# A wait for the scan of state k ahead of GpSimd's product for state k+3, in the state space stage of a two-layer decoder

## The chip, the cores and the metric

The kernel runs on one core of a Trainium2 chip. Its time is the device time of one execution in microseconds (us); the median of several runs is compared. A core has five engines with queues of their own: TensorE (PE in the profile, its weight loads PEld), VectorE (DVE), ScalarE (ACT), GpSimd (POOL) and SyncE (SP), which here issues DMA. They are ordered only by semaphores.

## The reference, cut to what matters

The whole program is six sub-layers on x of 8 x 256 x 512, each followed by a layer norm of x plus its result: sliding window attention, quantised cross attention, a GELU layer, a selective state space, linear attention, and a mixture of experts. The change is in the state space, and there in the recurrence over the 256 tokens:

```
u = silu(xs);  A = -exp(A_log);  dbc = u @ W_x          # N = 16 states
delta = softplus(dbc[..., :dtr] @ W_dt + b_dt)
deltaA = exp(einsum('bld,dn->lbdn', delta, A))
deltaBu = einsum('bld,bln->lbdn', delta * u, Bm)
h = dA * h + dBu;  y_t = einsum('bdn,bn->bd', h, c)      # one step over tokens
y = ys.transpose(1, 0, 2) + u * D;  out = y * silu(r);  return out @ W_out + xs
```

## The kernel before, in words

The kernel goes through eight stages one after another; the state space is the sixth (`state_space`). It handles the 8 batches in a software pipeline. In one step n there are 16 iterations k, one for each of the 16 states of batch n; the other parts of the work (convolution and projections of the batches behind, gate, output and norm of the batch before) are spread in pieces over the same 16 iterations. Channels lie on the 128 partitions in KD = 4 groups, tokens along the row, so a tile is 128 x 1024 numbers in float32. States are counted through over all batches as c = 16 n + k (`chunk_of`), 128 in all.

Each state takes this way through the engines:

- ScalarE computes `decay[c]`, exp(delta times a), in 4 activations (L2185), up to two states ahead of the scan.
- GpSimd computes the driving term, du times b (`drive`, L2335), and writes it into `state[c % 4]`. In iteration k it issues the product for state k+3 (`DRIVE_LEAD` = 3).
- VectorE runs the scan over the tokens (L2383), reading `decay` and `state` and writing the state in place. It waits for both.
- TensorE transposes the scanned state into PSUM (`turn`, L1933), in two halves of four transposes; in its order, the transposes of state k-1 come at the beginning of iteration k, ahead of that iteration's piece of the projections.
- VectorE adds the transposed state times c to an accumulator in two halves (L2394, `add_up`); in iteration k it does so for state k-2, right after scan k.

The state tiles form a ring of RING = 4. So the product for state c may overwrite its tile only when the transposes of state c-4 have been read from it; that is the wait on `turn_ready` in `drive`, which is there for all states from the fifth on. `scanned` is raised by each scan's end; until now TensorE and ScalarE wait for it.

Other work stands in the same queues. GpSimd in iteration 2 multiplies the accumulator of the batch before by its gate (L2346), and in iteration 11 computes the norm's inverse root and offsets (L82, L2358). VectorE in iterations 8 and 10 forms y (L2410) with its statistics (L1754), after iteration 10 also the moments, and at the end of iteration 12 makes delta (L2420) and du (L2423) for the next batch; the first product of that batch waits for du. Each engine runs its instructions strictly in the order written. `g.sem_inc(waited, 1)` behind a wait is only the instruction that carries the wait.

Of the kernel before, what the change touches and what calls it, by code (L numbers as in the profile page):

```python
# [35 lines left out]
ONE = 1  # L36
# [42 lines left out]
def inverse_root(g, ln, n):  # L79

    g.wait_ge(ln.shifted_ready, ONE + n + 1)
    g.tensor_tensor(ln.rstd[:, :], ln.shifted[:, :], ln.minus_half[:, :], ALU.pow).then_inc(ln.rstd_ready, 1)  # L82
# [17 lines left out]
def flat(a):  # L100

    return a.rearrange("p a b -> p (a b)")


def spread(row, n):

    return row.rearrange("p (o d) -> p o d", o=1).to_broadcast([P, n, row.shape[-1]])
# [1588 lines left out]
def state_space(nc, A, x_in, x_out, hold):  # L1696
# [9 lines left out]
    DRIVE_LEAD = 3  # L1706
    SUM_LAG = 2
    CONV_B, OUT_T, X_T, Y0, DT_B, C_T, Y1, Z, XC, SKIP, XC1, GATE, CONV_A = 0, 1, 3, 5, 6, 7, 8, 9, 11, 12, 14, 15, 17
    with Phase(nc, "ss", "right") as p:
# [108 lines left out]
        def run(eng, step):  # L1818

            step(-1, 0, False, False, False, True)  # L1820
            step(-1, 1, False, False, True, True)
            step(0, 0, False, True, True, True)
            with eng.Fori(0, (B - 4) // 2) as pair:
                step(pair, 1, True, True, True, True)
                step(pair + 1, 0, True, True, True, True)
            h = B // 2
            step(h - 2, 1, True, True, True, True)
            step(h - 1, 0, True, True, True, False)
            step(h - 1, 1, True, True, False, False)
            step(h, 0, True, False, False, False)  # L1830
# [13 lines left out]
        def wait_read(eng, q, s, j):  # L1844
            eng.wait_ge(freed[place(s, j)], ONE + used(q, s, j) + 1)

        def chunk_of(q, s, k):

            return q * (2 * N) + s * N + k
# [462 lines left out]
        @block.gpsimd  # L2312
        def _(g):
            behind.late_pool(g)
            g.memset(ln.minus_half[:, :], -0.5).then_inc(ln.half_set, 1)
            g.wait_ge(ln.half_set, ONE + 1)
            g.wait_ge(consts, ONE + 80)
            for m in range(KD):
                ins = g.tensor_scalar(diag[:, m, :], ident[:, :], skip[:, m:m + 1], None, ALU.mult)
            ins.then_inc(diag_ready, 1)  # L2320

            def step(q, s, post, back, mid, front):
                n = q * 2 + s

                def drive(q, s, k):
                    c = chunk_of(q, s, k)
                    if k == 0:
                        g.wait_ge(du_ready, ONE + q * 2 + s + 1)
                        g.sem_inc(waited, 1)
                        g.wait_ge(b_in, ONE + 16 * (q * 2 + s + 1))  # L2330
                        g.sem_inc(waited, 1)
                    if not (isinstance(q, int) and c < RING):
                        g.wait_ge(turn_ready, ONE + (c - RING + 1) * TB)
                        g.sem_inc(waited, 1)
                    g.tensor_tensor(state[k % RING][:, :, :], du[s][:, :, :], spread(b_all[s][:, k, :], KD), ALU.mult)\  # L2335
                        .then_inc(drive_ready, 1)

                for k in range(N):
                    if k == 2 and post:
                        last = (q - 1, s)  # L2340
                        g.wait_ge(summed, ONE + TB * chunk_of(q, s, 0))
                        g.sem_inc(waited, 1)
                        for t in range(TB):
                            wait_read(g, *last, GATE + t)
                            g.sem_inc(waited, 1)
                        g.tensor_tensor(flat(acc[1 - s][:, :, :]), flat(acc[1 - s][:, :, :]), flat(gate[1 - s][:, :, :]),  # L2346
                                        ALU.mult).then_inc(gated, 1)
                    if k + DRIVE_LEAD < N:
                        if back:
                            drive(q, s, k + DRIVE_LEAD)  # L2350
                    elif mid:
                        drive(q + s, 1 - s, k + DRIVE_LEAD - N)
                    if k == 11 and post and not (isinstance(q, int) and n == B):
                        inverse_root(g, ln, n - 1)
                        g.wait_ge(ln.rstd_ready, ONE + n)
                        g.sem_inc(waited, 1)
                        for t in range(TB):
                            ins = g.tensor_scalar(offset[:, t:t + 1], ln.moments[:, t, 0:1], -1.0, ln.rstd[:, t:t + 1],  # L2358
                                                  ALU.mult, ALU.mult)
                        ins.then_inc(offset_ready, 1)  # L2360

            run(g, step)
# [971 lines left out]
```

## Time and profile before

| | |
|---|---|
| median of 3 runs | 2904.63 us (2903.69 to 2905.1) |
| the profiled execution's own time | 2909.72 us |
| its span, first to last instruction | 2907.4 us |
| busy share of the span | PE 90%, PEld 61%, DVE 68%, ACT 50%, POOL 41% |
| mean granted TensorE clock | 0.964 |
| GpSimd's products (L2335) | 128, 433.3 us, mean 3395 ns |
| VectorE's scans (L2383) | 128, 386.9 us, mean 3023 ns |

The shares are averages over eight stages with different limits. The stage of the change lies between about 1690 and 2335 us. The stages are sequential, so what it gains or loses is gained or lost by the whole. An instruction counts as busy from its start to its end, also when it stands still in between.

### The profile page before, as it was taken

The numbers are of one execution on the slowest core, as the hardware profiler recorded it, in microseconds if no ns is written. First come the engines' busy times: TensorE is split into PE (matmuls) and PEld (weight loads), VectorE is DVE, ScalarE is ACT, GpSimd is POOL, SyncE is SP. The second block draws the span as 40 slices with busy tenths as digits, with TensorE's granted clock in tenths as the row PEclk, the third lists the DMA queues.
The fourth block names the chain that finished last, engine by engine and source line by source line (L and its number), as shares of the span: only waits on it lengthen the run. The fifth ranks groups of instructions, "written<-read, shape, count | busy, mean of one in ns | idle before, by whom it ended". The sixth has DMA issues, their size and how long they took to land. (4 is left out here: it accounts for less than half of the span.)

```text
span 2907.4 us, 47462 instructions
## 1 busy us (share of the span) xinstructions
PE 2623.1 (90%) x16930; PEld 1760.0 (61%) x16941; DVE 1988.6 (68%) x2548; ACT 1459.1 (50%) x2864; POOL 1206.2 (41%) x1148
## 2 busy tenths in 40 slices
PE   8999899988888888887999999999998879998997
PEld 5666655634444444443899777777776555555873
DVE  4788757689999999966121149999999933333544
ACT  3444422279999998972232156666676511111520
POOL 0000026446665665553222137776888810000352
PEclk9999999989999999999999999999999989998899
DMA  2123514268888888975012201111112270120273
GB/s 94 57 91 128 190 56 116 58 134 171 168 164 171 169 167 160 189 161 188 30 39 72 102 37 52 59 59 59 59 52 81 85 130 23 43 81 8 98 153 146
DMA packets 537722, 297.99 MB, mean 102 GB/s; under 512 B 444400, under 2 KB 482544, under 8 KB 533680
## 3 DMA queue, kind: packets, MB, share of 16 engines
q1 hardware_dynamic: 520896, 258.50, 35.4%
q0 software_dynamic: 16624, 36.84, 4.1%
q8 instruction: 122, 2.00, 0.3%
q14 instruction: 80, 0.66, 0.1%
HBM read 126.45 MB, written 64.23 MB: 66 GB/s over the span
## 5 line engine op out<-in xcount | busy, mean ns | idle before, releaser
L1188 DVE TENSOR_REDUCE xh_top<-xh_seen 128x1 f32<-128x512 f32 (+1 forms) x768 | 631.6, 864 | 44.1 <-PE xh_seen L1090 30.5
L1160 ACT ACTIVATE xh_prob<-xh_sc,xh_bias,xh_scale 128x1024 int16<-128x1024 f32 (+1 forms) x512 | 610.1, 1202 | 67.4 <-PE xh_sc L1090 67.1
L2335 POOL TENSOR_TENSOR ss_state<-ss_du,ss_b_all 128x1024 f32<-128x1024 f32 x128 | 433.3, 3395 | 185.2 <-PE ss_turned L1933 110.8
L1090 PE MATMUL xh_seen<-xh_kT,xh_qT 96*128 96x512 bf16 x1024 | 353.3, 387 | 80.4 <-DVE xh_top L1188 78.1
L2383 DVE TENSOR_TENSOR_SCAN ss_state<-ss_decay,ss_state 128x1024 f32<-128x1024 f32 x128 | 386.9, 3023 | 28.7 <-ACT ss_decay L2185 28.7
L1090 PE MATMUL xh_sc<-xh_kT,xh_qT 96*128 96x512 bf16 x1024 | 308.1, 383 | 1.4 <-ACT xh_prob L1160 1.3
L1214 POOL CAST xh_probT<-xh_pairs 128x2048 int16<-128x2048 uint8 x128 | 242.1, 1891 | 12.6 <-DMA xh_pairs<-xh_prob 3.8
L1090 PEld LDWEIGHTS xh_seen<-xh_kT,xh_qT 96*128 96x128 bf16 x1024 | 89.2, 97 | 240.8 <-DVE xh_top L1188 219.2
L1940 PE MATMUL ss_bank<-ss_xc,hold_w_conv 128*128 128x256 f32 x1024 | 229.3, 379 | 0.7 <-ACT ss_xc L2197 0.7
L2185 ACT ACTIVATE ss_decay<-ss_delta,ss_a 128x255 f32<-128x255 f32 x512 | 210.7, 496 | 0.4
L1940 PEld LDWEIGHTS ss_bank<-ss_xc,hold_w_conv 128*128 128x128 f32 x1024 | 190.0, 189 | 26.4 <-ACT ss_xc L2197 1.1
L1114 PEld LDWEIGHTS xh_o<-xh_v_head,xh_probT 128*128 128x128 f16 x4096 | 133.9, 96 | 84.5 <-POOL xh_probT L1214 38.8
L1228 POOL TENSOR_SCALAR xh_low<-xh_top 128x1 f32<-128x1 f32 x256 | 93.1, 364 | 207.4 <-DVE xh_top L1188 206.9
L2394 DVE SCALAR_TENSOR_TENSOR ss_acc<-ss_turned,ss_c_t,ss_acc 128x512 f32<-128x512 f32 x256 | 176.4, 729 | 1.1 <-PE ss_turned L1933 1.1
L1933 PE MATMUL ss_turned<-ss_ident,ss_state 128*128 128x128 f32 x1024 | 138.6, 277 | 34.8 <-DVE ss_acc L2394 33.1
L1933 PEld LDWEIGHTS ss_turned<-ss_ident,ss_state 128*128 128x128 f32 x1024 | 118.8, 143 | 60.5 <-DVE ss_state L2383 30.3
L1114 PE MATMUL xh_o<-xh_v_head,xh_probT 128*128 128x32 bf16 x4096 | 142.3, 177 | 14.3 <-DVE xo_heads_out L1177 8.3
L1090 PEld LDWEIGHTS xh_sc<-xh_kT,xh_qT 96*128 96x128 bf16 x1024 | 96.1, 98 | 77.3 <-ACT xh_prob L1160 4.6
L82 POOL TENSOR_TENSOR la_rstd<-la_shifted,la_minus_half 128x2 f32<-128x2 f32 x8 | 5.6, 694 | 318.9 <-DVE la_shifted L71 318.9
L1676 DVE TENSOR_TENSOR gf_e<-gf_y_psum,gf_b 128x1024 f16<-128x1024 f32 x8 | 9.8, 1225 | 185.0 <-PE gf_y_psum L1631 185.0
L1616 PE MATMUL gf_hid_psum<-gf_xT,gf_w 128*128 128x256 f32 x1024 | 126.6, 286 | 8.8 <-POOL gf_xT L1574 8.8
L1616 PEld LDWEIGHTS gf_hid_psum<-gf_xT,gf_w 128*128 128x128 f32 x1024 | 126.3, 195 | 9.8 <-issue 9.2
(399 smaller groups left out, 4767.8 us busy)
## 6 DMA issues: line engine op xcount, KB each, us to landing
ex_rows_in<-sa_unused POOLq DMA_DIRECT2D x18, 1088.0 KB, 5.2
ss_b_all<-ss_states SPq DMA_DIRECT2D x8, 2048.0 KB, 7.2
xa_kT<-xp_kT SPq DMA_DIRECT2D x8, 768.0 KB, 5.2
xh_qT<-xa_qT SPq DMA_DIRECT2D x48, 128.0 KB, 3.2
xh_kT<-xa_kT SPq DMA_DIRECT2D x48, 128.0 KB, 3.4
sa_x<-in_x SPq DMA_DIRECT2D x8, 512.0 KB, 3.8
sa_y<-in_x SPq DMA_DIRECT2D x8, 512.0 KB, 6.6
x_after_self_attention<-sa_y_out SPq DMA_DIRECT2D x8, 512.0 KB, 6.1
```

The lines of the kernel that those rows point to most:

```text
L1090: ins = pe.matmul(out[:, c * D:(c + 1) * D], qT[s][:, t * P:(t + 1) * P], kT[s][:, at + c * D:at + (c + 1) * D], start=True, stop=True)
L1114: ins = pe.matmul(o[:, t, :], probT[t % RING][:, b, :].bitcast(F16), v_head[s][:, b, :], start=(b == 0), stop=(b == TT - 1))
L1160: act.activation(out, scores, ACT.Exp, bias=bias[t % RING][:, :], scale=scale[s][:, t:t + 1], accum_out=total[s][:, half, t:t + 1]).then_i ...
L1188: ins = v.tensor_reduce(top[t % RING][:, k:k + 1], scores[:, 0:n], AX.X, ALU.max)\
L1214: g.tensor_copy(probT[t % RING][:, :, :].rearrange("p (b two) q -> p b two q", two=2), pairs[t % RING][:, :, :].bitcast(U8).rearrange("p b ...
L1616: ins = pe.matmul(hid_psum[m // 2 % 3][:, m % 2, :], w0[i][:, c, m * P:(m + 1) * P], xT[:, c, :], start=(c == 0 and i == 0), stop=(c == KD ...
L1933: ins = pe.transpose(turned[r][:, m * P:(m + 1) * P], state[k % RING][:, m, t * P:(t + 1) * P], ident[:, :])
L1940: ins = pe.matmul(out, w_conv[:, k, c, m * P:(m + 1) * P], xc[:, c, k:k + S], start=(k == 0 and c == 0), stop=(k == TAPS - 1 and c == KD - 1))
L2185: ins = act.activation(decay[k % RING][:, m, 1:], delta[s][:, m, 1:], ACT.Exp, scale=a[:, m, k:k + 1])
L2335: g.tensor_tensor(state[k % RING][:, :, :], du[s][:, :, :], spread(b_all[s][:, k, :], KD), ALU.mult)\
L2383: v.tensor_tensor_scan(flat(state[k % RING][:, :, :]), flat(decay[k % RING][:, :, :]), flat(state[k % RING][:, :, :]), 0.0, ALU.mult, ALU. ...
L2394: v.scalar_tensor_tensor(acc[s][:, t, :], turned[(k * TB + t) % BANKS][:, :], c_t[s][:, t, k:k + 1], acc[s][:, t, :], ALU.mult, ALU.add).t ...
```

## The change

The product for state c, from the fifth state on, waits for a second thing: that the scan of state c-3 has ended. With c = k+3 in iteration k, that is the scan of the same iteration on VectorE. The wait has its own carrying instruction.

```diff
@@ -2332,6 +2332,8 @@
                     if not (isinstance(q, int) and c < RING):
                         g.wait_ge(turn_ready, ONE + (c - RING + 1) * TB)
                         g.sem_inc(waited, 1)
+                        g.wait_ge(scanned, ONE + c - DRIVE_LEAD + 1)
+                        g.sem_inc(waited, 1)
                     g.tensor_tensor(state[k % RING][:, :, :], du[s][:, :, :], spread(b_all[s][:, k, :], KD), ALU.mult)\
                         .then_inc(drive_ready, 1)
```

## Rows read from the trace of the kernel before

**Rows 1.** Windows of one 16-state period; us, busy by engine, clock, DMA.

```profile
1783.50:1863.40 79.90, 77.22 (x418) 61.94 (x417) 75.20 (x59) 53.76 (x111) 53.91 (x21) 1.00 0.14 54
1941.95:2021.70 79.75, 77.13 (x417) 61.59 (x416) 75.20 (x59) 53.48 (x110) 54.44 (x21) 1.00 0.14 54
2100.20:2178.70 78.50, 75.45 (x410) 60.48 (x409) 75.08 (x59) 52.06 (x107) 65.37 (x21) 1.00 0.13 48
```

**Rows 2.** Waits from 1700 to 2330 us: total, times, longest.

```profile
POOL ss_state L2335 <- PE ss_turned L1933: 110.8, 52, 6.0
PE ss_turned L1933 <- DVE ss_acc L2394: 33.1, 17, 3.1
DVE ss_state L2383 <- ACT ss_decay L2185: 28.7, 16, 3.5
```

**Rows 3.** VectorE in order of time: start, us, instruction, idle before and releaser.

```profile
1881.57 3.68 DVE L2383 TENSOR_TENSOR_SCAN ss_state<-ss_decay,ss_state 128x1024 f32<-128x1024 f32 x1 [1.66 <-ACT ss_decay L2185]
1900.76 4.05 DVE L2383 TENSOR_TENSOR_SCAN ss_state<-ss_decay,ss_state 128x1024 f32<-128x1024 f32 x1 [1.29 <-ACT ss_decay L2185]
```

**Rows 4.** The scan's line: shortest, median, longest ns; then its group.

```profile
L2383 DVE TENSOR_TENSOR_SCAN ss_state<-ss_decay,ss_state x128: 2259/3087/4460, 1704.5 to 2325.2; 128x1024 f32<-128x1024 f32 x128
L2383 DVE TENSOR_TENSOR_SCAN ss_state<-ss_decay,ss_state 128x1024 f32<-128x1024 f32 x128 | 386.9, 3023 | 28.7 <-ACT ss_decay L2185 28.7
```

**Rows 5.** VectorE in order of time, 1907 to 1930 us.

```profile
1907.47 2.27 DVE L2383 TENSOR_TENSOR_SCAN ss_state<-ss_decay,ss_state 128x1024 f32<-128x1024 f32 x1
...
1910.96 3.10 DVE L2383 TENSOR_TENSOR_SCAN ss_state<-ss_decay,ss_state 128x1024 f32<-128x1024 f32 x1
...
1917.41 2.29 DVE L2383 TENSOR_TENSOR_SCAN ss_state<-ss_decay,ss_state 128x1024 f32<-128x1024 f32 x1
...
1925.24 3.40 DVE L2420 TENSOR_TENSOR ss_delta<-ss_delta,ss_soft 128x1024 f32<-128x1024 f32 x1
1928.67 1.23 DVE L2423 TENSOR_TENSOR ss_du<-ss_delta,ss_u 128x1024 f32<-128x1024 f32 x1
```

**Rows 6.** GpSimd in order of time, 1876 to 1931 us.

```profile
1876.42 4.35 POOL L2346 TENSOR_TENSOR ss_acc<-ss_acc,ss_gate 128x1024 f32<-128x1024 f32 x1
...
1909.09 2.81 POOL L2335 TENSOR_TENSOR ss_state<-ss_du,ss_b_all 128x1024 f32<-128x1024 f32 x1 [2.12 <-PE ss_turned L1933]
1914.29 2.37 POOL L2335 TENSOR_TENSOR ss_state<-ss_du,ss_b_all 128x1024 f32<-128x1024 f32 x1 [2.38 <-PE ss_turned L1933]
...
1925.18 2.37 POOL L2335 TENSOR_TENSOR ss_state<-ss_du,ss_b_all 128x1024 f32<-128x1024 f32 x1
1930.42 3.84 POOL L2335 TENSOR_TENSOR ss_state<-ss_du,ss_b_all 128x1024 f32<-128x1024 f32 x1 [2.87 <-DVE ss_du L2423]
```

**Rows 7.** GpSimd in the first batch: the first product issued early.

```profile
1732.06 2.37 POOL L2335 TENSOR_TENSOR ss_state<-ss_du,ss_b_all 128x1024 f32<-128x1024 f32 x1 [1.96 <-PE ss_turned L1933]
```

**Rows 8.** The last batch: a backlog, the last early product, a long scan.

```profile
2270.26 28.23 POOL L2335 TENSOR_TENSOR ss_state<-ss_du,ss_b_all 128x1024 f32<-128x1024 f32 x7
2308.45 4.21 POOL L2335 TENSOR_TENSOR ss_state<-ss_du,ss_b_all 128x1024 f32<-128x1024 f32 x1 [1.34 <-PE ss_turned L1933]
2316.03 4.46 DVE L2383 TENSOR_TENSOR_SCAN ss_state<-ss_decay,ss_state 128x1024 f32<-128x1024 f32 x1
```

**Rows 9.** TensorE's transposes, 1913 to 1935 us.

```profile
1913.07 1.04 PE L1933 MATMUL ss_turned<-ss_ident,ss_state 128*128 128x128 f32 x8
...
1932.80 1.97 PE L1933 MATMUL ss_turned<-ss_ident,ss_state 128*128 128x128 f32 x8 [2.21 <-DVE ss_acc L2394]
```

**Rows 10.** A product just ahead of a scan, batch 1.

```profile
1830.94 2.36 POOL L2335 TENSOR_TENSOR ss_state<-ss_du,ss_b_all 128x1024 f32<-128x1024 f32 x1 [3.88 <-PE ss_turned L1933]
1831.04 4.40 DVE L2383 TENSOR_TENSOR_SCAN ss_state<-ss_decay,ss_state 128x1024 f32<-128x1024 f32 x1
```

**Rows 11.** delta and du with VectorE first, 2239 to 2245 us.

```profile
2239.91 1.21 DVE L2420 TENSOR_TENSOR ss_delta<-ss_delta,ss_soft 128x1024 f32<-128x1024 f32 x1
2241.15 3.26 DVE L2423 TENSOR_TENSOR ss_du<-ss_delta,ss_u 128x1024 f32<-128x1024 f32 x1
```

## The prediction

> **What bounds the kernel now.** I read the stages by window first, because the change touches only one of the eight stages, the state space; it runs from about 1704 to 2335 us and handles 8 batches of 16 states. Three windows of one 16-state period each [rows 1] last from 78.5 to 79.9 us, with VectorE busy for 75.1 to 75.2 us, TensorE for 75.5 to 77.2, GpSimd for 54 to 65. Two engines are close to full, so busy time does not say which one sets the pace. The waits do [rows 2]: TensorE waits 33.1 us for VectorE's sums in 17 places, VectorE only 28.7 us for ScalarE's decays, and GpSimd 110.8 us for TensorE's transposes. The pace passes between them inside each batch. From about scan 8 of a batch to scan 13 VectorE runs without a gap and TensorE ends up waiting for it; from scan 14 to about scan 4 or 8 of the next batch TensorE runs without a gap and VectorE has spare time, which shows as its idle of 1.66 and 1.29 us ahead of two scans [rows 3].
>
> Next the durations, because VectorE's "busy" is partly waiting. One scan form, one shape, lasts from 2.26 to 4.46 us [rows 4], and one product form on GpSimd from 2.36 to 4.21 [rows 8, 10]. Followed in order of time, they exclude each other. The scan at 1907.47 meets no running product and takes 2.27 us, to 1909.74. The product that was issued inside it at 1909.09 ends at 1911.90, 2.16 us after that scan's end, though a product with nothing beside it takes 2.37 (1914.29). The next scan is issued at 1910.96, 0.94 us before that product's end, and lasts 3.10 us, to 1914.06: 2.16 us after the product's end [rows 5, 6]. So whoever comes second stands still, with its time counted as busy, until the first is done. The two sums between scans take the 1.22 us from 1909.74 to 1910.96 and do not care. A period is therefore scan, then product, with the sums hidden beside the product: 3.10 + 1.22 = 4.32 us. A scan met by nothing would be 2.27, and 128 of them are 96 us less than the 386.9 of [rows 4].
>
> **What the change does, step by step.** Nothing is removed and no DMA moves. GpSimd gets one more wait and one more counter increment ahead of each product from the fifth on, 124 in all. The product for state k+3 may now start only when scan k has ended.
>
> (1) *The products that this holds back.* I compared each product's start with the end of the scan it will wait for. In 57 cases the product is issued before that end, as at 1909.09 against 1909.74 [rows 5, 6]; the first such is at 1732.06, the last at 2308.45 [rows 7, 8]. In the other 67 the product is later anyway, held by the transposes or by its predecessor on GpSimd: after the gate product (L2346) GpSimd is one scan behind and runs seven products back to back, 28.23 us, 4.03 each [rows 8]. For these the scan named is already over, and the new wait is passed at once.
>
> (2) *The price of one that is held back.* It loses the place that it had while standing behind the scan. Now it ends 2.16 us after the scan. Afterwards the counter has to reach GpSimd and the whole instruction has to run. A product released by TensorE at 1914.11 (1913.07 + 1.04) starts at 1914.29, 0.18 us later [rows 6, 9]; released by VectorE's du at 1929.90 through three waits in a row it starts at 1930.42, 0.52 later, so some 0.17 per wait [rows 5, 6]. New end: 0.18 + 2.37 = 2.55 us after the scan, 0.39 us later than now. The next scan's length follows the product's end one to one, so 3.10 becomes 3.49 and the period 4.32 becomes 4.71. Bounds: 0 if a held product is taken as fast as a standing one; 0.56 (0.39 + 0.17) if the additional wait is paid after the scan too. I take 0.39, the row for one wait, because the older wait has been passed by then.
> Of the 57, 50 have a next scan that stands behind them; for the other 7 VectorE has y's sum and statistics in between (from 1914.06 to 1917.41, 3.35 us [rows 5]), which hides all of it. All 50 on the path would be 50 x 0.39 = 19.5 us.
>
> (3) *What of it lies on the path.* By batch the 50 are 8, 8, 5, 8, 5, 5, 5, 6.
> - First batch: VectorE has no spare time from scan 5 on, so 8 x 0.39 = 3.1 us.
> - Batches 2, 4, 5, 6: three of the five stand at scans 14, 15 and 0, where TensorE sets the pace; their 1.17 us go into the 1.66 us idle [rows 3]. The two at scans 10 and 12 are on the path: 0.78. But with scans 1.17 us later, the gate product ends later too, at about 1881.9 in place of 1880.77 (1876.42 + 4.35 [rows 6]), past the 1881.57 at which the scan is ready, and then GpSimd's catching up with two products in the gap no longer fits. That puts a part back. Between 0.78 and 5 x 0.39 = 1.95 I take 1.2 each, together 4.8.
> - Batches 1 and 3: five on the path, 1.95, less one gain: the product at 1830.94 starts 0.10 us before its scan (1831.04), which lasts 4.40 for it [rows 10]. With VectorE 1.5 us later by then, the product falls inside the scan before, stands there, and the scan is 3.1: 1.3 back. 0.7 each, together 1.4.
> - Last batch: little TensorE work, VectorE is waited for, 6 x 0.39 = 2.3. Its scan at 2316.03 comes 0.05 us after a product and lasts 4.46 [rows 8]. If the additional wait turns this order, 1.4 are saved; as even odds, 0.7. Leaves 1.6.
> Sum 3.1 + 4.8 + 1.4 + 1.6 = 10.9 us.
>
> (4) *Small ones.* Where products are back to back (seven in 28.23 us, nothing idle between [rows 8]) GpSimd passes its waits while the instruction before runs, and one more costs nothing. Where the transposes release the product the wait adds up to 0.17, some 15 times, 2.6 us if all of it were on the path; I take 0. At delta (L2420) product and VectorE tie: the product (1925.18) starts 0.06 us before it and delta lasts 3.40 with du 1.23, sum 4.63; in the batch at 2239.91 VectorE came first and the pair is 1.21 + 3.26 = 4.47 [rows 5, 6, 11]. Turning that tie gives 0.16 us a batch, below 1 us in all; 0. TensorE's idle grows by about 1 us at scan 13. After such a wait at 1932.80 the eight transposes took 1.97 us in place of 1.04, the lower of the clock's two levels [rows 9]; the batch that follows took 79.75 us against 78.50 for another [rows 1]. At none to four more such falls: 0 to 4.8 us; I take 0.
>
> **One rule weighed.** The rows show that the second of the two stands until the first is done. The Trainium skill, "SBUF — State Buffer", section "Who interferes with whom", says the same: the one that issues second is blocked completely until the other has finished. Taken literally this speaks for no cost at all: a product kept back until the scan's end loses nothing, as it was blocked until then, and the sum would be 0. By the rows the standing product ends 0.39 us earlier than a fresh one would, and the sum is 10.9.
>
> **The rivals.**
> *No change (2904.6; between 2898.8 and 2910.4).* About 0.2% is what a measurement of this kernel can tell, 5.8 us. Either the 0.39 is near 0 since a standing product is no faster than a fresh one, or idle of VectorE (28.7 us in all, some 3 a batch) takes the rest: 8 x 0.78 = 6.2 us would be left. For it: TensorE is at 96% of a batch. Against it: it waits for VectorE in every batch.
> *Faster (2896).* The mechanism is the order at near ties: a product that starts just before a scan costs it a whole product. 18 scans last over 3.5 us, together 72.1, which is 16.3 over 18 x 3.10. If delaying products and scans turns half of them, 8.2 us go: 2904.6 - 8.2 = 2896.4. It decides where a product starts less than 0.2 us ahead of a scan (0.10 us in one case, 0.05 in another [rows 8, 10]). Against it: most of the 18 are caused by GpSimd's backlog or by transposes, and the new wait starts nothing earlier.
> *Everything on the path and the clock with it (2929).* 19.5 + 4.8 = 24.3 us. For it: the two alternate without a gap, so that time in which neither runs is hard to get back.
> That the change does nothing because the wait is always passed already is excluded by the 57.
>
> **Numbers.** Forecast +10.9 on the profiled execution's 2909.72 gives 2920.6 (span 2907.4, to 2918.3); the median of the runs is 5.1 us below the profiled time, so 2904.63 + 10.9 = 2915.5 us. Chances: slower by my sum or thereabouts (2910.4 to 2924) 0.58, no change 0.27, faster 0.08, everything on the path 0.07. Range for 8 in 10: 2904 to 2926, of which the likeliest case's own is 2911 to 2922. Slower by over 0.2%: 0.65.
>
> **What would show it.** In the profile after: no product begins inside the scan that it is held by, so long products (3.5 to 4.4 us) grow rarer while GpSimd waits for the scan (L2383), a releaser that is absent now; a group of scans at 3.4 to 3.5 us beside those at 3.1; the scans' total up by more than 10 us; gaps of about 0.18 us from scan's end to product's start. Batches of some 79 to 80 us. The forecast is wrong if scans keep at 3.1 us behind a held product (price), if VectorE's idle for the decays shrinks by as much as the scans grow (cover), or if the number of scans over 3.5 us falls by half (order).

## The result, and the profile after

The changed kernel is slower: median 2924.83 us (2920.53 to 2932.93, 4 runs) against 2904.86; the medians are 20.0 us apart, the ratio is 1.0073, 95% interval 1.0049 to 1.0096. In a second measurement of the same kernel it is 1.0059 (1.0038 to 1.0079). The direction was forecast, the size was not: I had 10.9 us, these ratios are 21 and 17. The profiled execution took 2920.53 us, its span is 2918.6.

Other stages scatter by more than this change is worth (from the first to the last matmul of the experts it is 213 to 218 us in nine of the seventeen profiles of this document, 230 to 247 in the other eight), so I read the stage itself: from the start of the first scan to the start of the last it took 620.7 us before and 636.3 after; in a second profile of each, 618.6 and 634.8. That is 15.9 us on average, 0.55% of the kernel, inside both intervals.

The two groups and the waits of the stage in the kernel after, as in [rows 2, 4]; the line numbers are two higher from the added lines on.

```profile
L2385 DVE TENSOR_TENSOR_SCAN ss_state<-ss_decay,ss_state 128x1024 f32<-128x1024 f32 x128 | 402.1, 3142 | 28.8 <-ACT ss_decay L2185 28.7
L2337 POOL TENSOR_TENSOR ss_state<-ss_du,ss_b_all 128x1024 f32<-128x1024 f32 x128 | 379.9, 2981 | 253.9 <-DVE ss_state L2385 146.1 <-DVE ss_du L2425 54.8 <-PE ss_turned L1933 53.0
```

```profile
POOL ss_state L2337 <- DVE ss_state L2385: 146.1, 53, 4.7
PE ss_turned L1933 <- DVE ss_acc L2396: 39.4, 17, 3.5
DVE ss_state L2385 <- ACT ss_decay L2185: 28.7, 14, 3.4
```

GpSimd's line looks better by 53 us (433.3 before), and that is no gain: time in which it stood behind scans, counted as busy, is now shown as waiting for them, in 53 places. (Of the 146.1 us of that wait another part was a wait for the transposes before, which fell from 110.8 to 53.0.) The line that counts is VectorE's: its scans are 15.2 us longer in sum. Its idle for the decays is the same 28.7 us in this pair of profiles. In the second pair the scans are 22.1 us longer and that idle falls from 28.0 to 23.2, so there spare time did take some of it; the stage grows by about 16 us in both. TensorE waits longer for VectorE (39.4 against 33.1).

The same place as [rows 5], in order of time: VectorE of the kernel after, then GpSimd.

```profile
1914.34 2.27 DVE L2385 TENSOR_TENSOR_SCAN ss_state<-ss_decay,ss_state 128x1024 f32<-128x1024 f32 x1
...
1917.83 3.48 DVE L2385 TENSOR_TENSOR_SCAN ss_state<-ss_decay,ss_state 128x1024 f32<-128x1024 f32 x1
...
1932.88 3.39 DVE L2422 TENSOR_TENSOR ss_delta<-ss_delta,ss_soft 128x1024 f32<-128x1024 f32 x1
```

```profile
1887.59 21.94 POOL L2337 TENSOR_TENSOR ss_state<-ss_du,ss_b_all 128x1024 f32<-128x1024 f32 x6
...
1916.79 2.37 POOL L2337 TENSOR_TENSOR ss_state<-ss_du,ss_b_all 128x1024 f32<-128x1024 f32 x1 [2.58 <-DVE ss_state L2385]
...
1932.81 2.38 POOL L2337 TENSOR_TENSOR ss_state<-ss_du,ss_b_all 128x1024 f32<-128x1024 f32 x1
```

The scan at 1914.34 ends at 1916.61; the product starts at 1916.79, 0.18 us later, and ends at 1919.16, 2.55 us after the scan. The scan issued at 1917.83 lasts 3.48 in place of 3.10. After the next scan there is y's work in between, and the scan behind it (1924.66) takes 2.29 as before: nothing lost. The six products from 1887.59 stand back to back as before. At delta the product still comes 0.07 us first. Over all 128 scans, 47 now last 3.4 to 3.5 us (none before), 38 last 3.0 to 3.15 (76 before), and 12 last over 3.5 (18 before). In the second pair of profiles the first two counts are much the same (45 against 1, 37 against 77), but the third is 17 against 16.

TensorE at the end of that batch, beside [rows 9]:

```profile
1940.43 1.97 PE L1933 MATMUL ss_turned<-ss_ident,ss_state 128*128 128x128 f32 x8 [2.38 <-DVE ss_acc L2396]
1942.19 4.27 PE L2071 MATMUL ss_bank<-hold_w_in,ss_xT 128*128 128x512 f32 x8
```

It has waited, and the granted clock is at its lower level (1.2 of 2.4 GHz): 0.51 in the mean from 1940.1 to 1943.5. The transposes take 1.97 in place of 1.04, the matmuls behind them 4.27 in place of the 3.60 of the same eight in `after_busy2`, where the clock is not lowered.

**The stage by batch.** The table is the time from the start of scan 13 of one batch to that of the next, worked out from VectorE's rows in order of time; the first column runs from the first scan to scan 13 of batch 0, the last from scan 13 of batch 6 to the last scan of all. "Middle" is the sum of the six between, taken before they are rounded. A star marks a batch in which the clock fell to 1.2 GHz right at its start (in the last part it falls in every profile).

```
                   first   0-1   1-2   2-3   3-4   4-5   5-6    last   middle  whole
before              66.9  79.9* 78.6  79.7* 78.6  78.5  77.8    80.9   472.9   620.7
before, again       66.9  78.6  79.8* 78.5  78.5  78.5  77.8    79.9   471.7   618.6
after               71.1  80.4* 80.4* 80.4* 80.5* 79.5  80.3*   83.6   481.6   636.3
after, again        71.0  80.4* 79.7  80.6* 79.6  80.3* 79.4    83.6   480.1   634.8
```

### The profile page after: what moved, and what is told of

Read it like the earlier page. It is cut to its first block and busy times, and to the rows that moved or that the text cites. A ratio compares the mean times of both kernels' runs of the same rounds, so it can differ in the third digit from the quotient of the medians.

```text
span 2918.6 us, 47659 instructions
## 1 busy us (share of the span) xinstructions
PE 2629.8 (90%) x16941; PEld 1763.4 (60%) x16941; DVE 2003.7 (69%) x2548; ACT 1458.4 (50%) x2864; POOL 1151.5 (39%) x1148
## 5 line engine op out<-in xcount | busy, mean ns | idle before, releaser
L1160 ACT ACTIVATE xh_prob<-xh_sc,xh_bias,xh_scale 128x1024 int16<-128x1024 f32 (+1 forms) x512 | 609.8, 1202 | 67.3 <-PE xh_sc L1090 66.9
L2337 POOL TENSOR_TENSOR ss_state<-ss_du,ss_b_all 128x1024 f32<-128x1024 f32 x128 | 379.9, 2981 | 253.9 <-DVE ss_state L2385 146.1
L2385 DVE TENSOR_TENSOR_SCAN ss_state<-ss_decay,ss_state 128x1024 f32<-128x1024 f32 x128 | 402.1, 3142 | 28.8 <-ACT ss_decay L2185 28.7
L1933 PE MATMUL ss_turned<-ss_ident,ss_state 128*128 128x128 f32 x1024 | 142.2, 282 | 41.5 <-DVE ss_acc L2396 39.4
```

What stands on the lines that cost most here:

```text
L1160: act.activation(out, scores, ACT.Exp, bias=bias[t % RING][:, :], scale=scale[s][:, t:t + 1], accum_out=total[s][:, half, t:t + 1]).then_i ...
L1933: ins = pe.transpose(turned[r][:, m * P:(m + 1) * P], state[k % RING][:, m, t * P:(t + 1) * P], ident[:, :])
L2385: v.tensor_tensor_scan(flat(state[k % RING][:, :, :]), flat(decay[k % RING][:, :, :]), flat(state[k % RING][:, :, :]), 0.0, ALU.mult, ALU. ...
```

## The experiments

Each is told by the whole and by the parts of that table, since a few us in the stage are 0.1 to 0.3% of the kernel, near what the ratios can tell. The kernel before had medians of 2904 to 2931 us in these measurements, and not by the chip alone (chip 11 gave 2925.2 once and 2904.3 once); each ratio is against its runs in the same measurement.

**The change once more** (`again`, nothing edited).

> The changed kernel, unaltered, in more runs. The state space stage of its profile grew by about 16 us (from 2325.25 to 2340.76 at the last scan, with both traces laid on the first scan, and 1.0 before that), the median by 20. Theory: the held products cost 0.39 each and the rest above 16 us is scatter of the granted clock, so a median of 2917 to 2925 and a lowest near 2919. Rival (TensorE's longer idle brings regular falls of its clock, an effect of its own): runs spread from 2919 to 2933 with the granted clock falling from 0.963 to 0.957 as the time grows.

Ratio 1.0059 (1.0038 to 1.0079), 634.8 us in the stage. The stage repeats within 1.5 us. The median expected cannot be held against the 2944.13 measured, since the kernel before took 2925.24 there. Nor does the rival's pattern show: the six runs lie between 2943.0 and 2949.7, the granted clock between 0.956 and 0.961 in no order with them, and the kernel before scatters from 2919.7 to 2937.5 in this measurement too.

**The kernel before once more** (nothing edited).

> The kernel before, unaltered, for a second profile. Every theory: 620 to 622 us from first to last scan, as in the first profile (620.7), no scans at 3.4 to 3.5 us. If it is off by more than 1 us, differences of that size between batches mean nothing.

Ratio 1.0002 (0.9988 to 1.0017), 618.6 us in the stage: 2.1 under the first profile, a little more than the 1 us expected. The table says where: a fall of the clock in one middle batch in place of two, and 1.0 in the last part. There the near tie of [rows 8] has turned by itself: with nothing changed, the scan of state 13 of the last batch lasts 3.07 us in place of 4.46. The product that it meets, issued at 2316.14, comes while the scan before still runs (2314.52 to 2316.79) and stands behind that one.

```profile
2318.02 3.07 DVE L2383 TENSOR_TENSOR_SCAN ss_state<-ss_decay,ss_state 128x1024 f32<-128x1024 f32 x1
```

So differences of 1 us in a single batch are read only together with the stars, and against the mean of the two profiles.

**A wait that is always passed.**

```diff
-                        g.wait_ge(scanned, ONE + c - DRIVE_LEAD + 1)
+                        g.wait_ge(scanned, ONE + c - RING + 1)
```

> The added wait asks for the scan of state c-4 in place of c-3; the wait on the transposes of c-4 already implies it, so it is always passed and only its instructions are left. Theory (the price lies in giving up the place behind the scan): 0 to +2.6 us, products again issued inside the scan, scans at 3.08. Rival (the instructions themselves on GpSimd's queue cost it): more than half of the 20 us.

Ratio 0.9994 (0.9980 to 1.0008), 621.1 us in the stage, scans' median 3085 ns. The instructions of the wait do take time on GpSimd: behind a release by the transposes the product starts 0.28 or 0.34 us after it in place of 0.18. But nothing of this reaches the stage; a product that stands behind a scan ends 2.16 us after it all the same (the one at 1909.45 lasts 2.65 us, its like at 1909.09 in [rows 6] 2.81). What costs is what the added wait waits for.

**The wait for some states only.** `only_0_1_2`, `only_3_15`, `only_12_15`: the two added lines under `if k < 3:`, `if k >= 3:` or `if k >= 12:`, k being the product's own state.

> The added wait only for states 0, 1, 2 of a batch, whose products stand behind scans 13, 14 and 15. The prediction put these three under TensorE's pace: 0 to +2 us in all. Rival (they are on the path like the others): 3 x 7 x 0.39 = 8.2 us.

> The added wait for states 3 to 15 alone. The prediction: nearly all of the change's cost is here, +9 to +16 us. Rival (states 0 to 2 are on the path): +6 to +10, the two halves adding up to the whole.

> The added wait only for states 12 to 15, whose products stand behind scans 9 to 12, in the stretch that VectorE paces. The changed kernel is 15.6 us longer from first to last scan; states 3 to 15 alone gave 12.3, states 0 to 2 alone 3.0. Theory (only what stands in VectorE's stretch counts in the middle batches): two held products a batch on the path, 8 batches x 0.75 = 6 us, so 626 to 628 with middle batches 0.8 longer. Rival (place does not matter; every held product costs 0.39 wherever it is): the same number here, but then states 0 to 2 should have cost 7.8 rather than 3.0; it is told apart by the middle batches, which must then be no more than 0.8 longer in the changed kernel per two held.

```
                   first   0-1   1-2   2-3   3-4   4-5   5-6    last   middle  whole   ratio (95%)
states 0 to 2       66.9  79.0  79.7  79.0  79.0  79.7  78.3    82.0   474.7   623.7   1.0031 (1.0016-1.0047)
states 3 to 15      71.0  80.8  79.3  80.8  79.3  80.7  78.5    82.4   479.6   633.0   1.0053 (1.0034-1.0072)
states 12 to 15     68.3  79.3  79.3  80.1  79.3  79.2  80.1    81.7   477.4   627.4   1.0035 (1.0018-1.0053)
```

Against the mean of the two profiles before (619.7; first 66.9, middle 472.3, last 80.4) states 0 to 2 add 4.0 us and states 3 to 15 add 13.3; the whole change adds 15.9, so the two are nearly additive. States 0 to 2 hold back 21 products, 8.2 us worth at 0.39, and 4.0 arrive: 2.4 us in the middle batches, for 18 held products, and the rest in the last part. That the 18 lie under TensorE's pace in part was right, though 0 to 2 us was too low. States 12 to 15 add 7.7, of which 5.1 in the six middle batches, 0.8 each: two held products on the path. The forecast had 0.78. In the last part all three kernels have the near tie of [rows 8] as the first profile before has it (the scan lasts 4.45 to 4.46), so it is that profile's 80.9 that they compare with: before rounding, +1.2 for three held products, +1.5 for four, +0.8 for two, and +2.7 for seven in the whole change. There every held product costs its full 0.39. The three ratios are wider than these differences.

**The wait written twice.** The two added lines stand twice in a row, so that a product that was held back starts later still.

> The changed kernel with the added wait and its increment written twice, so that one more instruction lies between the scan's end and the product. From first scan to last the state space took 620.7 us before and 636.3 changed. Theory (the price is the time from the scan's end to the product's start, paid by the next scan): product 0.35 after the scan in place of 0.18, scans of 3.64 in place of 3.47, and some 45 x 0.17 = 7.7 us on top of 636 where on the path, 2 to 7 counting what idle hides. Rival (the cost is the loss of the order, whatever the delay): no more than 1 us on top.

GpSimd, then VectorE, of this kernel, first batch (the last row is the last batch's):

```profile
1738.59 2.36 POOL L2339 TENSOR_TENSOR ss_state<-ss_du,ss_b_all 128x1024 f32<-128x1024 f32 x1 [2.42 <-DVE ss_state L2387]
```

```profile
1734.76 3.56 DVE L2387 TENSOR_TENSOR_SCAN ss_state<-ss_decay,ss_state 128x1024 f32<-128x1024 f32 x1
...
2336.33 2.28 DVE L2387 TENSOR_TENSOR_SCAN ss_state<-ss_decay,ss_state 128x1024 f32<-128x1024 f32 x1
```

The additional wait puts the product 0.27 us after the scan's end (1738.32), not 0.35: one more costs 0.09 us here, not the 0.17 that I had from du. Scans take 3.56. The stage takes 638.6 us in the one profile (ratio 1.0073, 1.0055 to 1.0091, from two runs), 18.9 over before and 3.0 over the changed kernel, where 2 to 7 were expected. So the price per held product went from 0.39 to 0.48 and the cost from 15.9 to 18.9 us: 15.9 / 0.39 = 41 and 18.9 / 0.48 = 39. The cost goes with the delay, and some 40 held products' worth of it are on the path. In the last part the tie has turned here (the scan at 2336.33 lasts 2.28, that of the changed kernel 4.45; the next one 3.08 in place of 2.28), which gives 1.4 us back: 82.9 is less than the 83.6 of the changed kernel in spite of the higher price.

**TensorE kept busy in its idle.** Four (`busy`) or two (`busy2`) additional matmuls, whose result is overwritten by the gate's projection, ahead of the transposes of iteration 14; in the changed kernel and in the one before.

```diff
+                    if k == 14 and mid:
+                        out = fill(GATE + 1)
+                        for c in range(KD):      # range(2) in busy2
+                            pe.matmul(out[:, :], xT[1 - s][:, c, P:2 * P], w_in[:, c, D:2 * D], ...)
                     if k > 0 and back:
                         turn(q, s, k - 1)
```

> The changed kernel, and TensorE does four additional matmuls of 128x512 in iteration 14 ahead of its transposes, where it waits about 3 us for VectorE; what they write is overwritten by the gate's projection. They fill the idle after which its clock falls. Theory (clock): fewer low stretches than the 9 of the changed kernel in this stage and batches of 79.5 in place of 80.4 us, first to last scan 632 to 634. Rival (the clock costs nothing, VectorE alone sets the pace): 636 as before, however the clock stands.

> The kernel before with the same four matmuls. Theory (clock): the two batches of 79.7 and 79.9 us that follow a fall go to 78.6, first to last scan 618 to 619 in place of 620.7. Rival: unchanged, or longer by up to 1 us a batch if the matmuls outlast the idle of 2.2 us.

> The changed kernel with two additional matmuls of 128x512 (1.8 us) on TensorE ahead of the transposes of iteration 14, where it waits 2.4 us or more; what they write is overwritten. The six middle batches take 480.0 to 481.5 us in the changed kernel, 478.1 with four matmuls. Clock theory: 1 us or less of idle is left, no fall there, transposes at 1.04 us, batches all at 79.3 to 79.6, sum 476 to 478. Rival (VectorE alone sets the pace): 480 to 481.

> The kernel before with the same two matmuls. Its six middle batches take 471.7 and 473.1 us in two profiles, with one or two of them at 79.8 where the rest are at 78.5. Clock theory: none at 79.8, sum 470 to 471.5. Rival (the additional work delays TensorE, as four matmuls did: 476.1): above 473.

```
                   first   0-1   1-2   2-3   3-4   4-5   5-6    last   middle  whole   ratio (95%)
after, four         74.4  79.9  79.6  79.9  79.7  79.6  79.4    83.5   478.1   636.1   1.0051 (1.0033-1.0070)
before, four        70.4  79.2  79.3  79.7  79.4  79.3  79.2    79.9   476.0   626.4   1.0030 (1.0020-1.0040)
after, two          71.6  79.7  79.7  80.0  79.7  79.6  79.4    83.6   477.9   633.1   1.0050 (1.0029-1.0072)
before, two         68.6  78.6  78.6  78.6  78.6  78.5  77.8    80.0   470.5   619.1   0.9991 (0.9979-1.0002)
```

The added matmuls of the changed kernel, four and then two (each counts as two in the rows), and the transposes behind the two:

```profile
1938.12 3.60 PE L2158 MATMUL ss_bank<-hold_w_in,ss_xT 128*128 128x512 f32 x8
```

```profile
1936.70 1.88 PE L2158 MATMUL ss_bank<-hold_w_in,ss_xT 128*128 128x512 f32 x4
1939.77 1.31 PE L1933 MATMUL ss_turned<-ss_ident,ss_state 128*128 128x128 f32 x8 [1.19 <-DVE ss_acc L2401]
```

Four take 3.60 us, which outlasts the idle of the kernel before and costs it 3.7 us in the middle; for that question this pair was badly sized. They also make the first part 3.4 to 3.5 us longer in both kernels, so by the whole both expectations were missed (636.1 for 632 to 634, 626.4 for 618 to 619). The pair with two answers the question for the middle batches: no fall at the start of any of them in either kernel, and none in the kernel before at 79.8. (In the first part two matmuls still cost 1.7 and 0.6 us.) The clock's falls are worth 472.35 - 470.51 = 1.8 us there and 480.87 - 477.94 = 2.9 in the changed kernel (both sums lie where I expected them, the second only just; the transposes took 1.31 and not 1.04, at a granted clock of 1.00). The difference of the two kernels without falls is 477.94 - 470.51 = 7.4 us; with them it is 480.87 - 472.35 = 8.5. So in the middle batches the clock explains 1.1 us of the loss, and VectorE the rest. The first part has a fall of its own, of which more below.

**The gate product on VectorE**, in the kernel before: L2346 with its waits taken out of GpSimd's iteration 2 and put at the end of VectorE's iteration 1.

> The kernel before, with the gate product moved from GpSimd (iteration 2, L2346, 4.35 us) to VectorE (end of iteration 1), where it should take 1.2 us plus what it stands behind a product. Theory (scans and products share one place, and GpSimd's backlog after the gate makes the long scans at 3.7 and 4.0 us): backlog gone, fewer than 18 scans over 3.5 us, first to last scan 5 to 10 us under 620.7, all of it 0.2 to 0.4%. Rival (VectorE is full, so anything put there costs): 7 x 2 = 14 us longer.

Ratio 1.0001 (0.9990 to 1.0012), 619.6 us in the stage, 17 scans over 3.5 us. Both were wrong: it costs nothing and gains nothing that can be measured. The backlog is gone, and with it the long scans 4 and 8 (3.68 and 4.05 us in batch 2), but in the same batches scans 2 and 10 are long now (4.43 and 3.98). The collisions have moved.

**The product for state 15 behind du**, in the kernel before; then with the gate product on VectorE too; then in the changed kernel.

```diff
+                    if k == 12 and mid and back:
+                        g.wait_ge(du_ready, ONE + n + 2)
+                        g.sem_inc(waited, 1)
                     if k + DRIVE_LEAD < N:
                         if back:
                             drive(q, s, k + DRIVE_LEAD)
```

> The kernel before, with one wait more in each batch but at another place: the product for state 15 (iteration 12) waits for du, so that it no longer starts 0.06 us before delta and costs it 2.2 us. Theory (scans, delta, du and products take turns, and a product is free only where VectorE leaves a gap): delta 1.2 in place of 3.4, the product goes behind scan 13; 1 to 2 us less in a batch, 7 to 14 in all, 0.2 to 0.5%. Rival (the turn is only moved): the product pushed back makes a backlog that costs the same 2.2 at scans 14 to 2, so 0 to -2 us in all.

> The same with the gate product on VectorE too, so that the product pushed back does not meet GpSimd's backlog of the gate. That move alone gave 1.1 us from first to last scan. Theory: backlog gone, 10 to 18 us less than before from first to last scan. Rival: TensorE, busy 75.5 of 78.5 us in a batch, sets the pace as soon as VectorE is quicker, so no more than 3 us.

> The changed kernel, and the product for state 15 waits for du as well, as in the version that took 608.4 us from first to last scan in place of 619.7. Theory (the price of a held product and the collision at delta are separate): 635.6 - 11.3 = 624, scans at 3.47 still there. Rival (the backlog that follows the pushed product hides the new wait, since a product in a backlog is issued after the end it waits for): most of the price gone too, 612 to 618.

VectorE, then GpSimd, of the first of the three, at the end of iteration 12:

```profile
1919.90 1.21 DVE L2423 TENSOR_TENSOR ss_delta<-ss_delta,ss_soft 128x1024 f32<-128x1024 f32 x1
...
1922.28 2.29 DVE L2386 TENSOR_TENSOR_SCAN ss_state<-ss_decay,ss_state 128x1024 f32<-128x1024 f32 x1
```

```profile
1922.72 21.30 POOL L2335 TENSOR_TENSOR ss_state<-ss_du,ss_b_all 128x1024 f32<-128x1024 f32 x5 [2.84 <-DVE ss_du L2426]
```

```
                   first   0-1   1-2   2-3   3-4   4-5   5-6    last   middle  whole   ratio (95%)
p15_du              66.1  76.6  76.6  76.6  76.6  76.5  77.3    82.2   460.1   608.4   0.9958 (0.9942-0.9974)
p15_du_gate         66.1  76.3  76.6  76.3  76.4  76.2  77.6    82.5   459.4   608.0   0.9971 (0.9958-0.9984)
after_p15           69.8  77.3  77.3  77.9  77.4  77.3  77.2    84.0   464.4   618.2   1.0003 (0.9987-1.0020)
```

The first of the three beats both kernels: 11.3 us less in the stage (7 to 14 were expected), and a ratio 0.42% under 1. Delta takes 1.21 in place of 3.40, and the product pushed back stands behind the next scan, which it costs nothing. The batches lie at 76.6, near TensorE's busy 75.5, and none of the middle ones shows a fall of the clock at its start; by the pair with two matmuls I estimate that the absence of falls is 1.8 of the 11.3 us. The last part is 1.8 us longer. The gate product on VectorE adds nothing to it (11.7 us less, inside the 10 to 18 expected, but none of it by that move). In the changed kernel the same three lines bring 17.4 us (635.6 to 618.2); the held products' price is down from 15.9 to 9.8, with 21 scans at 3.4 to 3.5 us in place of 47. I had 624 with the two separate, or 612 to 618 with the price mostly gone. It is in between, at the edge of the second: in the backlog that follows the pushed product, products are issued after the end that they wait for, and those pay nothing.

## Why the prediction was wrong in its size

- **Step 1, which products are held back: right in kind, one short.** 57 were counted, 50 with a scan behind them. By the rows of the kernel before it is 58 and 51: the last batch has seven such products, not six. The trace after has 53 waits of GpSimd for a scan, and 47 scans of 3.4 to 3.5 us.
- **Step 2, the price: right.** 0.39 was forecast, from 0.18 for the release and 2.37 for a fresh product; 0.18, 2.37 and scans of 3.45 to 3.49 were measured. Of its bounds, 0 is excluded; one more wait costs 0.09 behind a scan's release, but 0.10 or 0.16 behind a release by the transposes, so the 0.17 taken from du was not far off there. With a wait that is passed the stage pays nothing, as step 4 had it. The rule that was weighed, taken literally, gave a cost of 0; for the standing product the rows were right.
- **Step 3, what lies on the path: here it failed.** 10.9 us at 0.39 are 28 held products; the measured 15.9 are 41, and the wait written twice says 39. By its terms:
  - First batch: 3.1 forecast, 4.1 measured. I priced each scan by what it was before. But the scan at 1758.06 lasts 4.28 us (3.23 before): its product was released by TensorE, not by a scan, and no longer early enough, at 1757.80, 0.26 us ahead of the scan. And where the last product meets delta, 0.4 us came on top that I had not followed. TensorE was late there by a fall of the clock that the forecast did not have: it waits 2.95 us for VectorE, the granted clock is 0.50 from 1749.0 to 1752.4 (1.00 before), and eight matmuls take 3.27 us in place of 1.89. Both profiles of the changed kernel have this fall in that wait, and neither of the kernel before has it there (in the second the clock falls at 1757.8, and the part still takes 66.9). 1.4 us earlier the transposes would have been done before the scan ahead of the product ended (1756.84); the product would have started at 1757.02, and the scan would last 3.47 like its neighbours. So by this estimate up to 0.8 of the 4.1 us comes from the clock. No run separates it.
  - Middle batches: 6.2 forecast (4.8 + 1.4), 8.5 measured. Without the falls of the clock it is 7.4. For a range of 0.78 to 1.95 a batch, 1.2 was near, except in batch 6, which is 2.0 longer (1.6 without falls); the term for more falls, which I took as 0, is 1.1 us net, since the kernel before has falls as well. The gain that I had put into batches 1 and 3 came (their scans of 4.40 and 4.32 us last 3.48), but it belongs to the batches that begin with a fall: in the second profile before, the one such batch is batch 2, and the scan of 4.39 is there.
  - Last batch: 1.6 forecast, 3.2 measured, half of it missed. I took six held products less 0.7 for a tie that might turn. There are seven, longer by 0.38 to 0.40 each, 2.7 us, and that is all of 83.6 - 80.9, the difference to the first profile before. The tie did not turn in the changed kernel: the scan is at 4.45 us (4.46 before). But it is not fixed: it had turned in the second profile of the kernel before, which lowers the mean before by 0.5 and makes up the rest of the 3.2, and it has turned with the wait written twice. That I gave it even odds was a guess, and it says nothing on what the wait does.
- **The rivals.** "No change" fails on the price. "Faster" needed near ties to turn. The scans over 3.5 us are 12 in place of 18 in the first pair of profiles, but 17 and 16 in the second, so no drop is shown that repeats; the single gains, as in batches 1 and 3, are in the sum above. "Everything on the path and the clock", 24.3 us, is too much by 8: states 0 to 2 cost about a third of their price in the middle batches, so there is cover. The clock's falls are real: 1.1 us net in the middle, and by the estimate up to 0.8 in the first part, of the 4.8 that I had as their bound.
- **The distance between stage and kernel.** The ratios 1.0073 and 1.0059 mean 21 and 17 us, the stage shows 15.9. Both intervals contain it. Whether 1 to 5 us more lie elsewhere, the runs do not tell.

The rows of the kernel after for the two places named: VectorE's, GpSimd's, and TensorE's of the first place, then the same matmuls of the kernel before:

```profile
1758.06 4.28 DVE L2385 TENSOR_TENSOR_SCAN ss_state<-ss_decay,ss_state 128x1024 f32<-128x1024 f32 x1
...
2332.60 4.45 DVE L2385 TENSOR_TENSOR_SCAN ss_state<-ss_decay,ss_state 128x1024 f32<-128x1024 f32 x1
```

```profile
1757.80 2.39 POOL L2337 TENSOR_TENSOR ss_state<-ss_du,ss_b_all 128x1024 f32<-128x1024 f32 x1 [3.11 <-PE ss_turned L1933]
...
2332.53 2.37 POOL L2337 TENSOR_TENSOR ss_state<-ss_du,ss_b_all 128x1024 f32<-128x1024 f32 x1
```

```profile
1748.25 1.56 PE L1933 MATMUL ss_turned<-ss_ident,ss_state 128*128 128x128 f32 x8 [2.95 <-DVE ss_acc L2396]
1749.61 3.27 PE L1946 MATMUL ss_bank<-ss_u,ss_w_x 128*128 128x256 f32 x8
...
1756.45 2.40 PE L1933 MATMUL ss_turned<-ss_ident,ss_state 128*128 128x128 f32 x16
```

```profile
1747.07 1.89 PE L1946 MATMUL ss_bank<-ss_u,ss_w_x 128*128 128x256 f32 x8
```

## What to carry to other kernels

Where two engines exclude each other as these two do, an instruction that is already issued and stands behind the other is in the best place: a wait that holds it back until the other is done only adds the release and the start to every turn, here 0.39 us. Look instead for the instruction that starts just ahead of a longer run of the other engine, as the product did 0.06 us ahead of delta, and push that one behind the run. And when an engine is slowed at fifty places, do not take the trace of before for the cover: count how many of the places have idle behind them in the same batch, and ask what the delay does to the third engine, whose longer waits can bring a lower clock. Take a second profile of the kernel before as well: a near tie of 0.05 us stood one way in the first and the other way in the second, and was worth 1 us.

## What the runs showed of the hardware that I had not expected

- An instruction of GpSimd that stands behind a scan of VectorE ends 2.16 us after the scan, though it lasts 2.37 us alone and 2.55 with the release, as if 0.2 us of its start were done while it stands.
- One more wait on GpSimd between release and product costs 0.09 us behind a scan's release (0.18 to 0.27), and 0.10 or 0.16 behind a release by the transposes (0.18 to 0.28 or 0.34), though what it asks for has long been met. None of this reached the stage's time where the product then stood behind a scan (`wait_passed`, ratio 0.9994).
- Waits of TensorE of about 2 us at the same place of each batch are followed by a fall of the clock in some batches and not in others (in five of the six middle ones in one profile of the changed kernel, in three in the other), and the batches that start with one are 0.6 to 1.4 us longer than the others of the same profile, batch 6 left aside. With 1.9 us of matmuls in the wait, 1.2 us or less of it left, there was none at these places.
